# Bias matmuls on eight small tiles of the array, a second log table, and regions of 14 tiles in place of 15

## The reference, cut to what matters

```python
# x: 16 heads x 1024 x 1024 (t rows, s columns), f32
rel = tril(t - s)                                    # distance, 0 above the diagonal
pos = max(rel.max(axis=-1), |L * init_L|)            # one number for each row
nd  = log(|c * rel| + 1) / (log(|c * pos| + 1) + 1e-6)
h   = relu(nd[..., None] * W1[0] + b1)               # 32 hidden values for each (t, s)
x   = x + (h @ W2 + b2).transpose(2, 0, 1)           # bias: 32 -> 16 heads
# then heads are mixed: one 16x16 matrix for each column s, one for each row t
ret = x @ (w + eye) + (x . qw1) qw2 + (x . kw1) kw2 + x * qdd + x * kdd
```

## Time and profile before

| | us |
|---|---|
| median of 3 runs | 911.21 |
| lowest and highest | 910.2, 916.39 |
| span of the profiled execution | 930.2 |
| PE busy in it | 741.4 |
| DVE, ACT, POOL busy | 452.3, 387.6, 432.9 |

### The profile page before, as it was taken

The page is one execution under the profiler, slowest core; times in us unless marked ns, Lnnn a source line. Parts: engine busy times, 40 slices in busy tenths (PEclk is TensorE's granted clock), DMA queues, the critical chain, the costliest instruction groups (busy, mean ns, idle before and its releaser), DMA issues. The chain is left out here.

```text
span 930.2 us, 39085 instructions
## 1 busy us (share of the span) xinstructions
PE 741.4 (80%) x18210; PEld 547.7 (59%) x18210; DVE 452.3 (49%) x483; ACT 387.6 (42%) x412; POOL 432.9 (47%) x267
## 2 busy tenths in 40 slices
PE   0678864798678876898799978999689878897984
PEld 0255654576556655666557745677357645676974
DVE  7496522376345533564346524464336524464352
ACT  3958624553463435543433334344233342341200
POOL 3545421254233432365458745586358753581020
PEclk9888887999999999999999999999899988999997
DMA  6787687658975999587976898488875988589068
GB/s 132 183 172 140 147 180 167 145 100 190 194 180 125 183 184 201 124 183 161 223 156 129 174 181 192 94 172 172 182 162 110 199 178 151 106 176 227 5 155 200
DMA packets 301055, 149.63 MB, mean 161 GB/s; under 512 B 30045, under 2 KB 296669, under 8 KB 300893
## 3 DMA queue, kind: packets, MB, share of 16 engines
q1 hardware_dynamic: 231456, 113.56, 56.9%
q10 hardware_dynamic: 69436, 33.58, 17.0%
HBM read 77.61 MB, written 69.47 MB: 158 GB/s over the span
## 5 line engine op out<-in xcount | busy, mean ns | idle before, releaser
L451 POOL TENSOR_TENSOR hidden<-log_table,row_scale 128x1024 f32<-128x1024 f32 x192 | 365.4, 1917 | 367.4 <-PE bias L757 359.5
L743 PE MATMUL main<-homes,mats_b 32*32 32x120 f32 (+1 forms) x9216 | 286.5, 272 | 119.6 <-issue 83.3
L743 PEld LDWEIGHTS main<-homes,mats_b 32*32 32x32 f32 x9216 | 257.9, 133 | 187.5 <-issue 136.1
L490 ACT ACTIVATE hidden<-hidden,b_col 128x1024 f32<-128x1024 f32 x192 | 220.3, 1149 | 310.3 <-POOL hidden L451 205.1
L732 PEld LDWEIGHTS main<-homes,mats_a 32*32 32x32 f32 x8192 | 238.1, 129 | 78.6 <-issue 54.9
L732 PE MATMUL main<-homes,mats_a 32*32 32x128 f32 x8192 | 258.8, 275 | 23.7 <-issue 23.6
L657 DVE SCALAR_TENSOR_TENSOR homes<-bias,b_col,homes 64x512 f32<-64x512 f32 (+1 forms) x256 | 185.8, 747 | 174.9 <-DMA homes<-in_x 106.5
L757 PE MATMUL bias<-hidden,w_blocks 128*64 128x512 f32 x768 | 207.6, 648 | 17.7 <-DVE b_col L620 8.8
L639 DVE TENSOR_TENSOR homes<-main,homes 128x1024 f32<-128x1024 f32 x128 | 156.8, 1225 | 107.7 <-PE main L732 104.6
L629 DVE COPY homes<-main 128x960 f32<-128x960 f32 x64 | 74.1, 1157 | 179.7 <-PE main L743 179.5
L517 ACT ACTIVATE homes<-main 128x960 f32<-128x960 f32 (+1 forms) x80 | 71.1, 891 | 109.4 <-PE main L743 99.3
(11 more groups left out here) (37 smaller groups left out, 32.2 us busy)
## 6 DMA issues: line engine op xcount, KB each, us to landing
homes<-in_x SPq DMA_DIRECT2D x200, 192.0 KB, 6.5
out_mixed<-homes ACTq DMA_DIRECT2D x104, 192.0 KB, 5.9
out_mixed<-homes SPq DMA_DIRECT2D x104, 192.0 KB, 5.6
homes<-in_x SPq DMA_DIRECT2D x72, 256.0 KB, 7.1
homes<-in_x SPq DMA_DIRECT2D x136, 64.0 KB
mats_in<-a_mats SPq DMA_DIRECT2D x128, 64.0 KB
out_mixed<-homes ACTq DMA_DIRECT2D x28, 256.0 KB, 8.0
out_mixed<-homes SPq DMA_DIRECT2D x28, 256.0 KB, 5.8
```

The source lines that it names most:

```text
L451: nc.gpsimd.tensor_tensor(hidden_tile(u, g).rearrange("p (j s) -> p j s", j=ROWS), bass.AP(logs.tensor, logs.offset, [list(logs.ap[0]), [1 ...
L490: nc.scalar.activation(hidden_tile(u, g), hidden_tile(u, g), ACT.Relu, bias=b1_col[:, 0:1])\
L743: mm = pe.matmul(main[of_group(g), i % 2, j * W:j * W + REGION_TILES[k] * ROWS], b_weights(g, C * ROWS + j), y_column(k, g, C * ROWS + j), ...
```

## The change

1. The bias matmuls. Before, one tile's bias was made with weights of 128 rows by 64 columns: two matmuls (one group) or four (two groups), each 512 wide. Now the array is used as tiles of 64 rows by 32 columns: the two slots of the lower 64 partitions and the two of the upper 64 each have weights of their own 64x32 (`w2_blocks` is now 128 x 32), and eight matmuls are issued, 256 wide (one group) or 512 wide (two groups). Each of the eight uses another part of the array. PSUM bank b (rows t of parity b) gets the lower half of `hidden` in quadrants (b, b+2) and the upper half in the others, so for odd rows the slots have to be exchanged.
2. A second log table, 1151 numbers for each partition, with the slots exchanged; POOL's multiply reads both tables through one four-dimensional pattern. It is made by one more DVE instruction, four more iotas, and an ACT logarithm over twice the numbers.
3. For tiles 0 to 63 `add_bias` reads PSUM in four instructions of 64x256 instead of two of 64x512.
4. To make room, a home has 14 tiles, not 15. Regions are now 8, eight times 14, and 8: ten instead of nine. The loads are pieces of 1, 3, 3, 3, 3, 1, the stores of 2, 3, 3, 3, 3, and the last region has three load pieces and stores of 2, 2, 2, 1, 1.
5. Some scratch of the setup moves to another home, and the constant of b1 is made with two matmuls instead of one.

```diff
-REGION_TILES = (8,) + (15,) * 8
+REGION_TILES = (8,) + (14,) * 8 + (8,)
-STORE_PIECES = {8: (2, 3, 3), 15: (2, 3, 3, 3, 4)}
-LAST_STORES = (2, 3, 3, 3, 2, 1, 1)
-LOAD_PIECES = {8: (1, 3, 4), 15: (1, 3, 3, 3, 4, 1)}
+STORE_PIECES = {8: (2, 3, 3), 14: (2, 3, 3, 3, 3)}
+LAST_STORES = (2, 2, 2, 1, 1)
+LOAD_PIECES = {8: (1, 3, 4), 14: (1, 3, 3, 3, 3, 1)}
...
-        log_table = sb("log_table", [P, TABLE])
+        log_table = sb("log_table", [P, 2, TABLE])
-        w2_blocks = sb("w2_blocks", [P, 2, P // 2])
+        w2_blocks = sb("w2_blocks", [P, GP])
...
+        def quadrant(q):
+            return slice(GP * q, GP * (q + 1))
...
                     nc.gpsimd.tensor_tensor(
-                        hidden_tile(u, g).rearrange("p (j s) -> p j s", j=ROWS),
-                        bass.AP(logs.tensor, logs.offset, [list(logs.ap[0]), [1, ROWS], [1, W]]),
-                        bass.AP(scales.tensor, scales.offset, [list(scales.ap[0]), [1, ROWS], [0, W]]),
+                        hidden_tile(u, g).rearrange("p (j b s) -> p j b s", b=2, s=W),
+                        bass.AP(log_table, t0 - SLOTS * W * g, [[2 * TABLE, P], [2, ROWS // 2], [TABLE + 1, 2], [1, W]]),
+                        bass.AP(row_scale, t0 % PART, [[PART, P], [2, ROWS // 2], [1, 2], [0, W]]),
                         ALU.mult).then_inc(nd_ready, 1)
...
                 for b in range(2):
-                    add = dve.scalar_tensor_tensor(
-                        out=y_rows(rows, k, T, b), in0=falling(u, b, 0 if both else b * (P // 2), P if both else P // 2),
-                        scalar=b2_col[rows, 0:1], in1=x_rows(rows, k, T, b), op0=ALU.add, op1=ALU.add)
+                    if groups_of(u) == 2:
+                        add = dve.scalar_tensor_tensor(
+                            out=y_rows(whole, k, T, b), in0=falling(u, b), scalar=b2_col[:, 0:1],
+                            in1=x_rows(whole, k, T, b), op0=ALU.add, op1=ALU.add)
+                        continue
+                    for part in range(2):
+                        some = slice(part * (ROWS // 4), (part + 1) * (ROWS // 4))
+                        add = dve.scalar_tensor_tensor(
+                            out=y_rows(low_half, k, T, b)[:, some], in0=falling_part(u, part, b),
+                            scalar=b2_col[low_half, 0:1], in1=x_rows(low_half, k, T, b)[:, some],
+                            op0=ALU.add, op1=ALU.add)
...
                 for b in range(2):
                     for g in range(groups):
-                        into = low_half if (g if groups == 2 else b) == 0 else high_half
-                        rows = hidden_tile(u, g).rearrange("p (j b s) -> p b j s", s=W, b=2)[:, b]
-                        mm = pe.matmul(bias[into, u % 2, b * BANK:(b + 1) * BANK], w2_blocks[:, g, :], rows,
-                                       start=True, stop=True)
+                        for part in range(3 - groups):
+                            for h, of in enumerate((low_half, high_half)):
+                                q = 2 * (g + part) + (h + b) % 2
+                                n = ROWS // 2 // (3 - groups)
+                                rows = hidden_tile(u, g)[of, :].rearrange("p (j b s) -> p b j s", s=W, b=2)
+                                mm = pe.matmul(bias[quadrant(q), u % 2, b * BANK:b * BANK + n * W], w2_blocks[of, :],
+                                               rows[:, b, part * n:(part + 1) * n, :], start=True, stop=True)
```

More of the change, by code:

```diff
@@ L86, in build @@
         zero_col = sb("zero_col", [P, 1])
-        slot_col = sb("slot_col", [P, 1])
+        slot_col = sb("slot_col", [P, 2])
         c_col = sb("c_col", [P, 1])
@@ L96, in build @@
         turned = term
-        first = {"a": spare_2[:, 6144:6400], "b": spare_2[:, 6400:6656]}
-        second = {"a": spare_2[:, 6656:6912], "b": spare_2[:, 6912:7168]}
+        first = {"a": spare_0[:, 3328:3584], "b": spare_0[:, 3584:3840]}
+        second = {"a": spare_0[:, 3840:4096], "b": spare_0[:, 4096:4352]}
         diag = {"a": spare_0[:, 2048:2176], "b": spare_0[:, 2176:2304]}
@@ L374, in _ @@
             for k in range(REGIONS):
-                while k + 1 < REGIONS and loaded[k + 1] < 5:
+                while k + 1 < REGIONS and loaded[k + 1] < min(5, len(load_pieces(k + 1))):
                     load_x(k + 1, loaded[k + 1])
@@ L389, in _ @@
                         load_mats_a(v)
-                    if k + 1 < REGIONS and T == min(6, REGION_TILES[k] - 4):
+                    if k + 1 < REGIONS and len(load_pieces(k + 1)) > 5 and T == min(6, REGION_TILES[k] - 4):
                         load_x(k + 1, 5)
@@ L394, in _ @@
                             store_upper(k, i)
-                    if k + 2 < REGIONS and T in (7, 10, 13):
+                    if k + 2 < REGIONS and T in (7, 10, 13) and loaded[k + 2] < len(load_pieces(k + 2)):
                         load_x(k + 2, loaded[k + 2])
@@ L402, in _ @@
         def _(pool):
-            nc.gpsimd.iota(log_table[:], pattern=[[1, TABLE]], base=-(W - 1), channel_multiplier=0,
+            nc.gpsimd.iota(log_table[:, 0, :], pattern=[[1, TABLE]], base=-(W - 1), channel_multiplier=0,
                            allow_small_or_imprecise_dtypes=True).then_inc(indices_made, 1)
@@ L406, in _ @@
             for q in range(SLOTS):
-                nc.gpsimd.iota(slot_col[HID * q:HID * (q + 1), :], pattern=[[1, 1]], base=W * q,
-                               channel_multiplier=0, allow_small_or_imprecise_dtypes=True).then_inc(indices_made, 1)
-            pool.wait_ge(indices_made, SLOTS + 1)
+                for odd in range(2):
+                    nc.gpsimd.iota(slot_col[HID * q:HID * (q + 1), odd:odd + 1], pattern=[[1, 1]],
+                                   base=W * ((q + GS * odd) % SLOTS), channel_multiplier=0,
+                                   allow_small_or_imprecise_dtypes=True).then_inc(indices_made, 1)
+            pool.wait_ge(indices_made, 2 * SLOTS + 1)
             nc.gpsimd.memset(ident, 0.0).then_inc(ident_made, 1)
@@ L611, in _ @@
             for q in range(SLOTS):
[L612 to L615, removed]
+                dve.tensor_copy(bass.AP(w2_blocks, HID * q * GP + q % GS, [[GP, HID], [GS, H]]),
+                                w2_rows[HID * q:HID * (q + 1), :]).then_inc(w2_placed, 1)
             compact("b")
@@ L639, in finish_tile, with falling, falling_part @@
                 dve.tensor_tensor(at, main[:, i % 2, :], at, ALU.add).then_inc(main_taken[i % 2], 1)
-            def falling(u, b, first_partition, partitions):
-                return bass.AP(bias, first_partition * 2 * COLS + u % 2 * COLS + b * BANK + W - 1,
-                               [[2 * COLS, partitions], [W, ROWS // 2], [-1, W]])
+            def falling(u, b):
+                return bass.AP(bias, u % 2 * COLS + b * BANK + W - 1, [[2 * COLS, P], [W, ROWS // 2], [-1, W]])
+            def falling_part(u, part, b):
+                return bass.AP(bias, part * (P // 2) * 2 * COLS + u % 2 * COLS + b * BANK + W - 1,
+                               [[2 * COLS, P // 2], [W, ROWS // 4], [-1, W]])
             def add_bias(k, T):
@@ L696, in _ @@
             pe.wait_ge(relu_b1_made, 1)
-            pe.matmul(bias[high_half, 1, 0:1], w2_blocks[:, 1, :], relu_b1[:, 0:1], start=True, stop=True)\
-              .then_inc(const_bias_made, 1)
+            for h, rows in enumerate((low_half, high_half)):
+                pe.matmul(bias[quadrant(GS + h), 1, 0:1], w2_blocks[rows, :], relu_b1[rows, 0:1], start=True, stop=True)\
+                  .then_inc(const_bias_made, 1)
             pe.wait_ge(const_bias_read, 1)
```

17 lines of the change are left out of this document (7 added, 10 removed).

## The result

The changed kernel takes 957.48 us (median of 4 runs, 955.07 to 958.84), the kernel before beside it 910.71 us (4 runs, 903.5 to 916.39): ratio 1.054, interval 1.048 to 1.060. Slower, as forecast, with 943 us forecast. Medians are of all executions, while ratios leave out those over 1.5% above the fastest of their kernel, so a ratio can differ from that of the medians by up to 1%.

The account below looks back on a forecast made before the run. It took SP's late DMA queue and PE's instruction packets, not PE's work, as the bound. 100 + 90 + 606 + 77 + 62 + 28 = 963 us of span, 943 us for the runs' median, range 900 to 965 us.

Parts of the forecast that it names:

- What bounds the kernel: Stages: 20 to 26 us each are not PE's work; SP's late DMA queue and stops at 128-matmul packets fill them.
- Eight at once: Bias tiles: eight matmuls run side by side, 1.08 us with two groups, 0.65 with one; packets go from 143 to 161.
- The second rival: Bias matmuls: row halves take turns at a PSUM bank, so the 83 us saved are nothing; 955 us, chance 0.10.
- What the saved work is worth: Bias in stages: saving eaten by packets with one group; with two, 0.7 us gained in B and 1 in A phase.
- A stage hardly gets shorter by its missing tile: Full stages: SP's queue has 82 DMAs for 83 at 1.08 us each, so 14 tiles save some 1.8 us.
- The sign that I named for late x: Stages: the x piece with tile 4 landing well before 79 us after the A phase's start would show the forecast wrong.
- The stages by number: Six stages between A phases: two with one group at 98 us, four with two at 102.5, together 606 us.
- The end: After the six stages: 77 us to the last full region's A phase, 62 for the new stage, 28 to finish.
- Setup and the first stage: Start: first A phase at 100 us, with 1 us for the second table and setup, then 90 to the second.
- DVE's term: Adds with one group: four instructions instead of two cost 0.3 us more a tile, put at 1 us a stage.
- factor of 0.98: Whole kernel: runs' median 911.21 us is 0.98 of the profiled 930.2 us span, so 33 us more becomes 32.
- The first rival: Whole kernel: PE's work decides, stages fall to 91.6 and 90.5 us, 880 us in all; chance 0.17.

Follow-up runs that it names:

- e3: Kernel before with every bias matmul split into four of 128 columns, same columns and four times the instructions; 984.46 us, ratio 1.082.
- e5: Kernel before with each B step as 16 matmuls of 64x64 instead of 32 of 32x32, B weights wrong; 882.76 us, ratio 0.970.
- e6: Kernel before with DVE's adds of tiles 0 to 63 in four instructions of 64x256 instead of two of 64x512; 915.07 us, ratio 0.999.
- e7: Changed kernel with every x load from region 3 on bringing only the first row of its piece; 868.41 us, ratio 0.955.
- e2: Kernel before with the new bias matmuls and four DVE adds, but one log table and regions of 15 tiles; 921.55 us, ratio 1.017.
- e11: Kernel before with the ring of hidden values, w2_blocks and relu(b1) in half precision; 894.37 us, ratio 0.986.
- e1: Kernel before with only the ten regions of the changed kernel and its load and store pieces; 949.83 us, ratio 1.048.
- e9: e5 with the ten regions of the changed kernel; 911.36 us, ratio 1.014 against the kernel before.
- e4: Kernel before with only groups 0 and 1 of four in every B step, halving its matmuls; 946.65 us, no ratio given.

## Why the prediction was right, and where it was off

*What bounds the kernel.* Right in the main: packets end PE's work every 128 matmuls (e3, e5, the rows of the short region). One of the sums that were to show it shows nothing: 91 + 37 and 25 + 103 are 128 because a bias tile comes every two steps of 64. What shows it is the distance from stop to stop, 37 + 8 + 83 = 128. The packets explain why the new bias alone is a loss. They don't explain the loss as a whole: 39 of 47 us come with the region more, and how much of that is theirs is open.

*Eight at once.* Right: 1.09 and 0.66 us were forecast as 1.08 and 0.65, 161 packets as 161. The second rival, the halves taking turns at a PSUM bank, is out; the rule in the Trainium skill (TensorEngine Tiling (Array Packing), Gotcha 1) does not hold for these tiles, which write different quadrants of a bank.

*What the saved work is worth.* I took 5 us of gain in one-group stages as eaten by packets. It was more than eaten: the new bias costs 6.1 us there alone and 5.5 with the new regions. For two groups I took 1.7 us of gain; alone it is 5.3 and with the new regions 0.4. In all the bias alone is a loss of 11 us (15 by the ratio), though 73 us of work are gone: 37 us went to longer and more stops on main and 18 to stops on the bias matmuls, the granted clock fell from 0.934 to 0.913, and A and B matmuls alone are busy 19 us more. I had not put the clock into the sum.

*A stage hardly gets shorter by its missing tile.* Wrong, and I had called it the heart of the forecast. The regions alone take 5.5 us off a stage with one group and 8.4 off one with two (2.7 and 6.8 against e6's trace), where I had 1.8. My error lies at SP's queue: I charged 1.08 us for every DMA and so nearly nothing for a tile less. In a stage of the changed kernel SP issues 84 DMAs in 83.1 us (671.32 to 754.93 us), against 80 in 86.7, and then stands idle for 14.6 us; its time does not follow the number of DMAs:

```profile
733.05 21.88 SPq L320 DMA_DIRECT2D homes<-in_x  x24
```

Before, the same 24 took 28.30 us. Nor does it follow the bytes: in a stage of e7, where the pieces of three tiles bring a third, 84 DMAs take 74.8 us and the 48 of x among them 41.0, against 44.5 in the changed kernel. What sets the queue's pace is open. The sign that I named for late x came as forecast, 745.14 - 666.22 = 78.9 us after the A phase's start, with 79 forecast:

```profile
745.14 1.41 DVE L661 SCALAR_TENSOR_TENSOR homes<-bias,b_col,homes 128x512 f32<-128x512 f32 x2 [1.73 <-DMA homes<-in_x]
```

*The stages by number.* With one group 98 us were forecast and 98.1 measured, and that is luck: the regions took off more than I had, and the bias put about as much on. With two groups 102.5 were forecast and 96.0 measured. This is the 26 us by which the six stages, forecast at 606 us, came in at 580.

*The end.* Wrong the other way: 77 + 62 + 28 = 167 us forecast, 190.3 measured. The A phase and B phase to the last full region's A phase took 90.5 (77 forecast), the next 72.6 (62). I had built both on stages without loads and on the columns' work; but most of the short B phase is paced by packets at 3.47 us, not by 2.09 us of work, and the one ahead of it still has x and stores in the queues (its stops are up to 5.66 us long). The two errors, 26 us too much and 23 too little, cancelled in the span: 963 forecast, 954.7 measured. That the number came close is luck too.

*Setup and the first stage:* 100 and 90 forecast, 97.6 and 86.7 measured. DVE's term: an add of 64x256 takes 480 ns, 0.4 us more a tile where I had 0.3, and it costs nothing (e6). POOL's: 1933 against 1917 ns a multiply.

*From the span to the runs.* The profiled execution of before was 19 us longer than its median; I carried this as a factor of 0.98. In truth a run is 1.8 us longer than its own span (956.54 and 954.7 us), so a span of 963 stands for 965 us, the edge of my range, and not for 943. The factor hid that the baseline was a long execution: I forecast 33 us more against it, and it was 24.5 against it and 47 against the median. The runs of before scatter from 895.5 to 926.7 us over all experiments.

*The first rival*, PE's work deciding, is out by e2 and e11: 73 us of work are worth less than nothing, 135 us 13.

*Open:* what the region more costs, beside its B phase. By the timelines of e1 and of before the end's 66 us are 32 for the short B phase, 17 for the A steps and bias tiles around it, and 16 for the stage ahead (92.4 in place of 76.4 us), likely because x of one more region is loaded beside it; the shorter stages give back a part. e9 didn't part packets from work, and moving the short region elsewhere was not tried.

## What to carry to other kernels

Count PE's instructions as well as its columns: where a timeline shows stops without a releaser at a fixed number of matmuls, the next saving is in fewer, larger matmuls, and a faster form that needs more of them may lose. An engine that is busy 80% is not the bound until one has seen what stands between its instructions: 135 us less work of PE gave 13 us here, and 27 us when the packets were fewer. A tail that is built from other phases' work needs its own bound by packets and loads. And before a forecast is built on one trace, its span should be held against the median of the runs: this one was 19 us long.

## What the hardware showed that was not expected

- A packet of 128 matmuls with their weight loads takes no less than 3.46 us, and 3.47 time after time with quiet DMAs (24% and 9% busy). In full stages stops one packet apart are 5.0 us apart in the median with less x (e7) and 6.3 with all of it (the changed kernel). Packets that were added cost 4.1 us each on average (e3), more where a bias tile has one group than where it has two.
- Halving the matmuls that run side by side lowered the mean granted clock from 0.934 to 0.817 (e4), with the same number of columns streamed by each tile of the array. With 64x64 tiles in place of 32x32, as few matmuls kept it at 0.945 (e5), where the runs of before beside it had 0.929 to 0.945.
- 64x64 matmuls take 66 ns each at 120 columns and 67 ns at 64 (e5), so the columns don't set their pace. Their weight loads take 215 ns on average against 133 ns for 32x32; that these set the pace is a guess, which no run tests.
- Eight matmuls of 64x32 and 512 columns take 1.09 us together, with both row halves writing one PSUM bank in different quadrants: what two of 128x64 took before.
